# Retention of a two-layer network: results kept heads by tokens, score groups over four banks, value products of eight heads in one visit

## Chip, cores, metric
One core of a Trainium2 chip runs the kernel. The time is the device time in microseconds (us) of one execution. All data are fp32.

## What is computed
`reference` applies two layers to x (32 x 256 x 128): first a mean-field attention with a gated feed-forward, then the layer that the change touches, a retention with 16 heads and a mixture of 8 experts with soft routing. The retention, cut to what matters:

```python
qk = x @ W_qk + b_qk;  v = x @ W_v + b_v              # 16 heads, 8 wide (q, k), 16 wide (v)
scores = einsum('bhtd,bhsd->bhts', q, k) * mask       # causal decay, divided by a row scale
denom = clip(abs(scores).sum(-1), 1.0, 50000.0)
ret = einsum('bhts,bhsv->bthv', scores / denom, v)
ret = ret * rsqrt(mean(ret * ret, -1) + EPS)          # over the 16 values of a head
gated = (x @ W_g + b_g) * ret.reshape(Bx, Tx, H * VD)
return gated @ W_o + b_o
```

Both the old and the new kernel use that dividing by `denom` and then normalizing is u / sqrt(mean(u*u) + EPS*denom*denom) for the undivided u.

## The kernel before
The sequences are worked on in 16 pairs, 512 tokens (4 tiles of 128) each. The steps of all stages are short functions, one per engine and step; the table `ORDER` lists for each engine the order of its steps as (name, index, age). `steps_of` runs through that list once per cycle, 18 times in all (`pairs + ages`), and a step of age 1 or 2 works on the pair of one or two cycles ago. So each engine interleaves the first layer of pair p with the second layer of pair p-1 and the end of pair p-2, in an order written out by hand. Every engine works its list strictly in order; semaphores (`filled`, `ready`) tie the lists together.

PSUM has four single banks, `banks`, which the steps share by the table `BANK`, and `bank_s` of four banks for the scores. `claim` (line 812) makes TensorE wait until the last step that used a bank has been read, by the table `READ_BY`.

The retention of a pair, before (32 units: 2 sequences with 16 heads; a group `q` of 4 heads, 8 groups):
- `qk`, `vg` (L908, L913): projections; `qkc` (L644, VectorE) adds the bias and the decay, `vgc` (L652, L654) puts values and gates into `vrow` and `grow`, tokens by heads. `km` (L323, GpSimd) masks k to one head of each 32-row group.
- `quad` (L990, L993, TensorE): scores of 4 heads at once, one per 32-row group, each into a bank of `bank_s`: 256 query columns for the first 128 keys, 128 columns for the second. `ret` (L661, VectorE) multiplies by the causal block into one of two buffers, `ab` (L485, ScalarE) takes the absolute value, `add` (L329, GpSimd) adds the parts of it.
- `g` (L1008, TensorE): per head and 32-column group, values times `ret` (256 and 128 columns) and a column of ones times `ret_abs` (256), 4 heads in a bank. `RTc` (L490) copies it out; `row` (L1018) turns four of these back to tokens by heads.
- `usq` (L495), `rowd` (L670 to L677) and `urs` (L334, a power -0.5 on GpSimd) make the factor per head and token; `gated` (L683), `gatedT` (L1027) turned again, `gTc` (L500), `o` (L1035) and `attn` (L691).
The expert part is `xn3T`, `LT` (L920), `DT` (L942), `slots` (L950), `h` (L959), `eo` (L969), `out` (L979) on TensorE with `LTc`, `DTe`, `Dc`, `slc`, `ce` and `hg` (L480, Gelu) on ScalarE, `LTm`, `mx`, `cs`, `hb` (L726), `eoc`, `z` on VectorE and `dn` (L340) on GpSimd. The first layer has `xnT`, `s`, `e`, `k`, `r`, `v`, `score`, `PT`, `srow`, `local`, `xn2T` on TensorE, and `mix` (L556) among VectorE's steps.

Of the kernel before, what the change touches and what calls it, by code (L numbers as in the profile page):

```python
# [32 lines left out]
def columns(*widths):  # L33
    out, at = {}, 0
    for name, n in widths:
# [25 lines left out]
           ("row", 2, 1), ("gatedT", 0, 1), ("row", 3, 1), ("out", 0, 1), ("xn2T", 0, 0), ("out", 1, 1)],  # L61
    "DVE": [("z", 1, 2), ("stat", 0, 0), ("qkc", 0, 1), ("qkc", 1, 1), ("gated", 2, 2), ("vgc", 0, 1),
            ("LTm", 0, 1), ("LTm", 1, 1), ("ret", 0, 1), ("drec", 0, 1), ("attn", 0, 2), ("gated", 3, 2),
            ("vgc", 1, 1), ("xn", 0, 0), ("drec", 1, 1), ("LTm", 2, 1), ("zg", 0, 2), ("ret", 1, 1),
            ("attn", 1, 2), ("mx", 0, 1), ("LTm", 3, 1), ("drec", 2, 1), ("vgc", 2, 1), ("mx", 1, 1), ("mx", 2, 1),
            ("drec", 3, 1), ("vgc", 3, 1), ("ret", 2, 1), ("rmax", 0, 1), ("ret", 3, 1), ("cs", 0, 1),
            ("cs", 1, 1), ("mix", 0, 0), ("cs", 2, 1), ("ret", 4, 1), ("gbias", 0, 0), ("hb", 0, 1),
            ("rowd", 0, 1), ("hb", 1, 1), ("ret", 5, 1), ("hb", 2, 1), ("rowd", 1, 1), ("hb", 3, 1), ("eoc", 0, 1),
            ("sg", 0, 2), ("hb", 4, 1), ("ka", 0, 0), ("smax", 0, 0), ("eoc", 1, 1), ("smax", 1, 0),
            ("gated", 0, 1), ("ret", 6, 1), ("srowc", 0, 0), ("hb", 5, 1), ("ret", 7, 1), ("rv", 0, 0),  # L70
# [55 lines left out]
def build(nc, x, weights, vectors, consts, w1, w2, slot_rows, out):  # L126
    pairs = x.shape[0] // TOK
    ages = max(age for order in ORDER.values() for _, _, age in order)
    with ExitStack() as ctx:
# [45 lines left out]
        RT = sb("RT", 4, SEQ)
        usq = sb("usq", 2, HEADS, VD)
        ug, gated = sb("ug", TILES, HEADS, VD), sb("gated", 2, HEADS * VD)
        ums, den, den2, uvar, urs = (sb(n, TILES, HEADS) for n in ("ums", "den", "den2", "uvar", "urs"))
        gatedT = sb("gatedT", 2, 2, 2, P)
# [943 lines left out]
```

## Time and profile before

| | |
|---|---|
| time, median of 3 runs | 1098.42 us (1098.21 to 1098.63) |
| profiled execution, its time / span | 1098.24 us / 1096.4 us |
| busy: TensorE, VectorE, ScalarE, GpSimd | 1062.8, 960.2, 773.0, 606.9 us |
| mean granted TensorE clock | 0.992 of full speed |

The engine names in rows: PE is the matmul side of TensorE, PEld its weight loads, DVE VectorE, ACT ScalarE, POOL GpSimd. A matrix product in fp32 leaves two records each for product and load; ends of products are modelled, so that the distance from one start to the next is what a step takes. L-numbers are lines of the kernel. In a row, `128*32 128x256` is stationary rows*columns, then what streams.

### The profile page before, as it was taken

How to read it: one execution, taken by the hardware profiler on the slowest of the kernel's cores; microseconds unless marked ns; L12 is line 12 of the kernel's file. 1: busy time of each engine (PE TensorE's matmuls, PEld its weight loads, DVE VectorE, ACT ScalarE, POOL GpSimd, SP SyncE). 2: the span in 40 equal slices, each digit the busy share in tenths (PEclk: the TensorE clock that was granted, in tenths of full speed). 3: DMA queues.
4: the chain of work that ended last, by engine and by line, in shares of the span. 5: the costliest groups of instructions: out<-in, count | busy, mean ns of one | idle time of the engine just before them, and what ended most of it. 6: DMA issues, size and time to landing. Idle time of an engine off the chain costs nothing.

```text
span 1096.4 us, 27975 instructions
## 1 busy us (share of the span) xinstructions
PE 1062.8 (97%) x10436; PEld 832.9 (76%) x10436; DVE 960.2 (88%) x2074; ACT 773.0 (71%) x1450; POOL 606.9 (55%) x619
## 2 busy tenths in 40 slices
PE   5799999999999999999999999999999999999997
PEld 3478687787868778687787868778687787868776
DVE  3788989899898988989899898988989899898985
ACT  3476786767777676786767777676786767777674
POOL 2465547556474665547556474655647556474553
PEclk9899999999999999999999999999999999999998
DMA  6000000000000000000000000000000000000000
GB/s 257 11 2 11 1 20 3 1 21 1 21 1 11 11 1 22 1 12 10 2 21 1 21 1 2 20 2 21 2 11 11 2 20 2 21 1 2 11 1 20
DMA packets 18468, 16.97 MB, mean 15 GB/s; under 512 B 800, under 2 KB 17440, under 8 KB 18080
## 3 DMA queue, kind: packets, MB, share of 16 engines
q1 hardware_dynamic: 18336, 15.18, 4.2%
q8 instruction: 86, 1.41, 0.6%
q14 instruction: 46, 0.38, 0.1%
HBM read 10.98 MB, written 4.19 MB: 14 GB/s over the span
## 4 chain that ended last, share of the span: by engine, by line
PE 90%; DVE 6%; issue 1%; ACT 1%; POOL 0%; POOLq 0%; DVEq 0%; ACTq 0%
PE bank L1008 12%; PE bank L959 11%; PE bank L969 10%; PE bank_s L990 7%; PE bank L950 5%; PE bank L979 5%; PE bank L920 5%; PE bank L913 5%; PE bank L1035 3%; DVE ret L661 3%; PE bank L908 3%; PE bank L823 3%; PE bank L874 3%; PE bank L1018 3%; PE bank_s L993 2%; PE bank L854 2%
## 5 line engine op out<-in xcount | busy, mean ns | idle before, releaser
L329 POOL TENSOR_TENSOR ret_abs<-ret_abs 128x512 f32<-128x512 f32 x128 | 168.7, 1318 | 238.2 <-ACT ret_abs L485 238.2
L661 DVE TENSOR_TENSOR ret<-bank_s,k_sb 128x1536 f32<-128x1536 f32 x128 | 223.9, 1749 | 23.7 <-PE bank L1008 14.8
L334 POOL TENSOR_TENSOR urs<-uvar,mhalf 128x16 f32<-128x16 f32 x64 | 185.3, 2903 | 91.8 <-DVE uvar L677 91.8
L485 ACT ACTIVATE ret_abs<-ret 128x1536 f32<-128x1536 f32 x128 | 189.6, 1481 | 8.8 <-DVE ret L661 8.8
L959 PE MATMUL bank<-slotsT,w_sb 128*128 128x128 f32 x1024 | 140.9, 281 | 0.3 <-DVE hact L726 0.3
L969 PEld LDWEIGHTS bank<-w_sb,hact 128*128 128x128 f32 x1024 | 125.5, 192 | 14.7 <-issue 13.9
L969 PE MATMUL bank<-w_sb,hact 128*128 128x128 f32 x1024 | 134.1, 277 | 0.0
L959 PEld LDWEIGHTS bank<-slotsT,w_sb 128*128 128x128 f32 x1024 | 124.3, 192 | 10.3 <-issue 7.4
L340 POOL TENSOR_SCALAR dT<-dT,drec 128x256 f32<-128x256 f32 x128 | 83.4, 665 | 48.6 <-DVE drec L721 48.4
L1008 PE MATMUL bank<-ret,vrow 128*32 128x256 f32 (+1 forms) x2048 | 108.6, 329 | 0.3 <-DVE hact L726 0.2
L990 PE MATMUL bank_s<-qT,km 32*128 32x256 f32 x1024 | 91.4, 426 | 5.0 <-DVE ret L661 5.0
L726 DVE TENSOR_TENSOR hact<-bank,v_sb 128x512 f32<-128x512 f32 x128 | 87.4, 684 | 6.7 <-PE bank L959 5.3
L1008 PEld LDWEIGHTS bank<-ret,vrow 128*32 128x32 f32 x2048 | 59.7, 109 | 42.7 <-issue 5.0
L480 ACT ACTIVATE hact<-hact 128x512 f32<-128x512 f32 x128 | 79.8, 624 | 8.1 <-DVE hact L726 7.8
L446 ACT ACTIVATE cT<-bank 128x512 f32<-128x512 f32 x64 | 38.2, 597 | 58.1 <-PE bank L920 55.8
L1008 PE MATMUL bank<-ret_abs,k_sb 128*32 128x256 f32 x1024 | 79.2, 379 | 0.0
L990 PEld LDWEIGHTS bank_s<-qT,km 32*128 32x128 f32 x1024 | 40.4, 183 | 50.4 <-issue 48.2
L490 ACT ACTIVATE RT<-bank 128x256 f32<-128x256 f32 x128 | 48.0, 375 | 40.6 <-PE bank L1008 40.6
L323 POOL TENSOR_SCALAR km<-kT,k_sb 128x256 f32<-128x256 f32 x128 | 69.5, 543 | 6.9 <-DVE kT L644 6.8
L913 PE MATMUL bank<-w_sb,xn2T 128*128 128x512 f32 x128 | 66.1, 598 | 0.0
L461 ACT ACTIVATE dT<-cT,ltmax 128x256 f32<-128x256 f32 x128 | 64.0, 509 | 0.0
L979 PE MATMUL bank<-eorow,cT 128*128 128x129 f32 x512 | 62.3, 275 | 0.0
(143 smaller groups left out, 2397.9 us busy)
## 6 DMA issues: line engine op xcount, KB each, us to landing
x_sb<-x SPq DMA_DIRECT2D x16, 256.0 KB, 2.8
w_sb<-w SPq DMA_DIRECT2D x2, 2048.0 KB, 14.8
out<-attn SPq DMA_DIRECT2D x16, 256.0 KB, 2.3
v_sb<-vectors SPq DMA_DIRECT2D x1, 832.0 KB, 8.1
w_sb<-weights SPq DMA_DIRECT2D x1, 512.0 KB, 5.3
k_sb<-consts SPq DMA_DIRECT2D x1, 466.0 KB, 6.6
w_sb<-weights SPq DMA_DIRECT2D x1, 320.0 KB, 3.2
slot_sb<-slot_rows SPq DMA_DIRECT2D x1, 256.0 KB, 3.5
```

Source lines behind the costliest of these rows:

```text
L329: pool.tensor_tensor(both[:, :, P:SEQ], both[:, :, P:SEQ], both[:, :, SEQ:3 * P], ALU.add)\
L334: pool.tensor_tensor(urs[:, j], uvar[:, j], mhalf[:], ALU.pow).then_inc(ready["urs"].sem, 1)
L340: ins = pool.tensor_scalar(dT[:, m % 2, b], dT[:, m % 2, b], drec[:, m, b:b + 1], 1.0, ALU.mult, ALU.mult)
L485: act.activation(ret_abs[:, q % MR], ret[:, q % MR], ACT.Abs).then_inc(ready["ab"].sem, 1)
L661: dve.tensor_tensor(ret[:, q % MR], bank_s[:, :, 0:3 * P], causal.unsqueeze(1).broadcast_to([P, Q, 3 * P]), ALU.mult)\
L726: dve.tensor_tensor(hact[:, e % 2], bank[:].rearrange("p (c n) -> p c n", c=HC), V["b1"][:, e * HC:(e + 1) * HC].unsqueeze(2).broadcast_to ...
L913: pe.matmul(bank[:], xn2T[:, j // 2, (j % 2) * P:(j % 2 + 1) * P], W["vg"], start=True, stop=True)\
L959: ins = pe.matmul(bank[:, c * P:(c + 1) * P], w1_sb[:, e, c * P:(c + 1) * P], slotsT[:, e // 2, 2 * (e % 2):2 * (e % 2) + 2].rearrange("p ...
L969: ins = pe.matmul(bank[:, i * C:(i + 1) * C], hact[:, i, c], w2_sb[:, e, c], start=(c == 0), stop=(c == HC - 1))
L979: ins = pe.matmul(bank[:, i * (C + 1):(i + 1) * (C + 1)], cT[:, m, j * P:(j + 1) * P], eorow[:, m, b], start=(m == 0), stop=(m == E // 2 - 1))
L990: pe.matmul(bank_s[:, n, 0:SEQ], km[rows, q % KM, 0:P], qT[par][rows, b], start=True, stop=True)
L1008: ins = pe.matmul(bank[n * HT:(n + 1) * HT, sblock * P:SEQ], left, src[:, q % MR, n, cols[0]:cols[1]], start=(phase == 0), stop=(phase == 2))
```

## The change
The retention is laid out anew, and the order of all engines with it.
- Scores: `scores` (named "A") comes in six visits per pair, three per sequence. The first fills `bank_s` with the 128-column parts of all 16 heads (`low`); the second and third with the 256-column parts of 8 heads each (`high`). `ret` and `ab` now handle 2048 elements per partition, in one buffer each; `add` handles 1024.
- Values: `values` ("gg") takes eight heads in one visit of a bank. A head has 16 rows: the left half of the bank holds u for 8 heads by 256 tokens, the right half the sum of |scores|, spread over the head's 16 rows. `row`, `RTc`, `gatedT`, `gTc` are gone; `gT` and `gTb` make the gates heads by tokens as well.
- Norm: `ms` multiplies the squares by a block matrix (1/16 within a head) into the right half; `den`, `dsq`, `rx` add EPS*denom^2; `ln` and `rs` form exp(-0.5 ln) on ScalarE for a whole pair at once, in place of the powers `urs` on GpSimd.
- The orders of PE, DVE, ACT and POOL and the table `BANK` are new. `xn2T`, `eo 6`, `eo 7` and `out` move to the start of the next cycle.

```diff
-    "PE": [("qk", 0, 1), ("xn3T", 0, 1), ("qk", 1, 1), ("vg", 0, 1), ("LT", 0, 1), ("LT", 1, 1), ("quad", 0, 1),
...
+    "PE": [("xn2T", 0, 1), ("eo", 6, 2), ("eo", 7, 2), ("qk", 0, 1), ("qk", 1, 1), ("out", 0, 2), ("xn3T", 0, 1),
+           ("out", 1, 2), ("LT", 0, 1), ("xnT", 0, 0), ("A", 0, 1), ("s", 0, 0), ("o", 0, 2), ("LT", 1, 1),
+           ("A", 1, 1), ("LT", 2, 1), ("vg", 0, 1), ("o", 1, 2), ("LT", 3, 1), ("k", 0, 0), ("gT", 0, 1),
+           ("gT", 1, 1), ("DT", 0, 1), ("DT", 1, 1), ("A", 2, 1), ("gg", 0, 1), ("DT", 2, 1), ("DT", 3, 1),
+           ("vg", 1, 1), ("slots", 0, 1), ("slots", 1, 1), ("global", 0, 0), ("ms", 0, 1), ("mxT", 0, 1),
+           ("h", 0, 1), ("gg", 1, 1), ("A", 3, 1), ("rB", 0, 1), ("e", 0, 0), ("h", 1, 1), ("r", 0, 0),
+           ("A", 4, 1), ("h", 2, 1), ("eo", 0, 1), ("h", 3, 1), ("eo", 1, 1), ("ms", 1, 1), ("score", 0, 0),
+           ("score", 1, 0), ("srow", 0, 0), ("A", 5, 1), ("gg", 2, 1), ("PT", 0, 0), ("PT", 1, 0), ("v", 0, 0),
+           ("eo", 2, 1), ("local", 0, 0), ("eo", 3, 1), ("ms", 2, 1), ("h", 4, 1), ("h", 5, 1), ("h", 6, 1),
+           ("gg", 3, 1), ("eo", 4, 1), ("h", 7, 1), ("eo", 5, 1), ("ms", 3, 1)],
...
+    "DVE": [("eoc", 2, 2), ("xn3", 0, 1), ("eoc", 3, 2), ("stat", 0, 0), ("qkc", 0, 1), ("qkc", 1, 1), ("z", 0, 2),
+            ("xn", 0, 0), ("gated", 0, 2), ("gated", 1, 2), ("z", 1, 2), ("LTm", 0, 1), ("ret", 0, 1),
+            ("mix", 0, 0), ("attn", 0, 2), ("drec", 0, 1), ("LTm", 1, 1), ("ret", 1, 1), ("drec", 1, 1),
+            ("vgc", 0, 1), ("zg", 0, 2), ("attn", 1, 2), ("LTm", 2, 1), ("sg", 0, 2), ("mx", 0, 1), ("LTm", 3, 1),
...
+    "ACT": [("hg", 7, 2), ("xn2Tc", 0, 1), ("ln", 0, 2), ("rs", 0, 2), ("xn3Tc", 0, 1), ("LTc", 0, 1),
+            ("xnTc", 0, 0), ("DTe", 0, 1), ("sT", 0, 0), ("zt", 0, 2), ("LTc", 1, 1), ("ab", 0, 1), ("DTe", 1, 1),
+            ("LTc", 2, 1), ("ab", 1, 1), ("kr", 0, 0), ("gTb", 0, 1), ("LTc", 3, 1), ("DTe", 2, 1), ("Dc", 0, 1),
...
-        ret, ret_abs = sb("ret", MR, Q, 3 * P), sb("ret_abs", MR, Q, 3 * P)
...
+        low, low_abs = sb("low", Q, Q, P), sb("low_abs", Q, Q, P)
+        high, high_abs = sb("high", Q, 2, SEQ), sb("high_abs", Q, 2, SEQ)
...
+            def ln(p, par, k):
+                act.wait_ge(*ready["rx"](p, DUOS - 1))
+                act.activation(rx[:], rx[:], ACT.Ln).then_inc(ready["ln"].sem, 1)
+
+            def rs(p, par, k):
+
+                act.wait_ge(*ready["ln"](p))
+                act.activation(rx[:], rx[:], ACT.Exp, scale=-0.5).then_inc(ready["rs"].sem, 1)
...
+            def ret_(p, par, a):
+                b, i = divmod(a, 3)
+                dve.wait_ge(*filled["A"](p, a))
...
+                    since(dve, filled["gg"], *((p, h - 1) if h else (p - 1, HALVES - 1)))
+                    ins = dve.tensor_tensor(high[:].rearrange("p n i m -> p (n i) m"), flat.rearrange("p (u m) -> p u m", m=SEQ),
+                                            causal[:, 0:SEQ].unsqueeze(1).broadcast_to([P, 2 * Q, SEQ]), ALU.mult)
...
+            def rx_(p, par, h):
+                dve.wait_ge(*filled["ms"](p, h))
+                dve.wait_ge(*ready["dsq"](p, h))
+                dve.wait_ge(*ready["ug"](p, h))
+                since(dve, ready["gated"], p - 1, h // 2)
+                dve.tensor_tensor(rx[:, h], banks[BANK["gg", h]][:, SEQ:], den[:, h % 2], ALU.add).then_inc(ready["rx"].sem, 1)
...
+                for u, q in enumerate(quads):
                     for n in range(Q):
-                        src = (ret, ret_abs)[phase // 2]
...
+                        rows = slice(n * HT, (n + 1) * HT)
+                        if i == 0:
+                            ins = pe.matmul(bank_s[:, n, u * P:(u + 1) * P], km[rows, q % KM, P:SEQ], qT[par][rows, b, P:SEQ],
+                                            start=True, stop=True)
+                        else:
+                            ins = pe.matmul(bank_s[:, n, u * SEQ:(u + 1) * SEQ], km[rows, q % KM, 0:P], qT[par][rows, b],
+                                            start=True, stop=True)
+                ins.then_inc(filled["A"].sem, 1)
...
+                for i in range(2):
+                    for phase in range(3):
+                        for n in range(Q):
...
+                            right = (high[:, n, i], low[:, n, 2 * half + i], high_abs[:, n, i])[phase]
+                            into = ((0, SEQ), (P, SEQ), (SEQ, 2 * SEQ))[phase]
+                            ins = pe.matmul(bank[n * HT:(n + 1) * HT, into[0]:into[1]], left, right,
+                                            start=(i == 0 and phase == 0), stop=(i == 1 and phase == 2))
...
+            def ms(p, par, h):
+                pe.wait_ge(*ready["den"](p, h))
+                pe.wait_ge(*ready["ug"](p, h))
+                pe.matmul(banks[BANK["gg", h]][:, SEQ:], K["heads"], usq[:, h % 2], start=True, stop=True)\
+                  .then_inc(filled["ms"].sem, 1)
```

## Rows read from the trace of the kernel before

**Rows 1.** The page: part 1 busy us of engines; part 2 granted clock.
```profile
PE 1062.8 (97%) x10436; PEld 832.9 (76%) x10436; DVE 960.2 (88%) x2074; ACT 773.0 (71%) x1450; POOL 606.9 (55%) x619
...
PEclk9899999999999999999999999999999999999998
```

**Rows 2.** Timeline of PE: start us, us, instructions; first `qk` of two cycles.
```profile
103.74 1.02 PE L908 MATMUL bank<-xn2T,w_sb 128*128 128x512 f32 x2
...
499.46 1.02 PE L908 MATMUL bank<-xn2T,w_sb 128*128 128x512 f32 x2
```

**Rows 3.** Two cycles: us, busy of PE, PEld, DVE, ACT, POOL; clock, DMA.
```profile
499.46:565.40 65.94, 65.67 (x655) 51.75 (x653) 59.75 (x129) 48.06 (x90) 37.75 (x39) 1.00 0.03 10
565.40:631.34 65.94, 65.65 (x652) 51.51 (x651) 59.65 (x127) 48.05 (x90) 37.51 (x39) 1.00 0.04 10
```

**Rows 4.** Waits of PE from 499 to 631 us: total us, times, longest.
```profile
PE bank_s L990 <- DVE ret L661: 0.5, 2, 0.3
```

**Rows 5.** Timeline of PE within the cycle from 499.46 us.
```profile
503.77 0.59 PE L920 MATMUL bank<-xn3T,slot_sb 128*128 128x256 f32 x2
504.30 0.71 PE L990 MATMUL bank_s<-qT,km 32*128 32x256 f32 x8
...
505.16 1.16 PE L1035 MATMUL bank<-w_sb,gatedT 128*128 128x128 f32 x8
...
520.05 0.71 PE L990 MATMUL bank_s<-qT,km 32*128 32x256 f32 x8 [0.28 <-DVE ret L661]
...
530.17 0.60 PE L1018 MATMUL bank<-k_sb,RT 128*128 128x128 f32 x4
530.62 1.13 PE L959 MATMUL bank<-slotsT,w_sb 128*128 128x128 f32 x8
...
543.78 0.86 PE L1008 MATMUL bank<-ret,vrow 128*32 128x256 f32 x16
...
546.08 1.16 PE L959 MATMUL bank<-slotsT,w_sb 128*128 128x128 f32 x8
```

**Rows 6.** Timeline of the weight loads in the same visit.
```profile
504.62 0.42 PEld L993 LDWEIGHTS bank_s<-qT,km 32*128 32x128 f32 x8
```

**Rows 7.** Groups by line, PE: records, busy us, mean ns | idle before.
```profile
L1018 PE MATMUL bank<-k_sb,RT 128*128 128x128 f32 x256 | 38.8, 274 | 0.0
...
L1027 PE MATMUL bank<-k_sb,gated 128*128 128x128 f32 x128 | 19.3, 273 | 1.7 <-DVE gated L683 1.7
```

**Rows 8.** Groups by line, the other engines.
```profile
L661 DVE TENSOR_TENSOR ret<-bank_s,k_sb 128x1536 f32<-128x1536 f32 x128 | 223.9, 1749 | 23.7 <-PE bank L1008 14.8 <-PE bank_s L993 8.9
L485 ACT ACTIVATE ret_abs<-ret 128x1536 f32<-128x1536 f32 x128 | 189.6, 1481 | 8.8 <-DVE ret L661 8.8
L334 POOL TENSOR_TENSOR urs<-uvar,mhalf 128x16 f32<-128x16 f32 x64 | 185.3, 2903 | 91.8 <-DVE uvar L677 91.8
L329 POOL TENSOR_TENSOR ret_abs<-ret_abs 128x512 f32<-128x512 f32 x128 | 168.7, 1318 | 238.2 <-ACT ret_abs L485 238.2
...
L726 DVE TENSOR_TENSOR hact<-bank,v_sb 128x512 f32<-128x512 f32 x128 | 87.4, 684 | 6.7 <-PE bank L959 5.3
...
L480 ACT ACTIVATE hact<-hact 128x512 f32<-128x512 f32 x128 | 79.8, 624 | 8.1 <-DVE hact L726 7.8
...
L480 ACT ACT_TABLE_LOAD x32 | 41.1, 1283 | 0.6
L455 ACT ACT_TABLE_LOAD x32 | 41.1, 1283 | 0.6
...
L671 DVE TENSOR_TENSOR ug<-bank,grow 128x256 f32<-128x256 f32 x64 | 26.5, 415 | 0.0
```

**Rows 9.** Instructions of line 556: ns shortest/median/longest, first and last start.
```profile
L556 DVE SCALAR_TENSOR_TENSOR mix<-xnT,v_sb,mix x32: 744/961/1752, 11.2 to 989.0; 128x512 f32<-128x512 f32 x32
```

**Rows 10.** The chain that ended last, near its end: start us, us.
```profile
1082.08 2.91 POOL urs L334
1084.99 2.88 POOLq L129
```

More of the change, by code:

```diff
@@ L50 @@
 ORDER = {
[10 rows of a table removed]
[L61 to L70, printed above, removed]
[3 rows of a table removed]
@@ L102 @@
+BANK = {("DT", 0): 3, ("DT", 1): 2, ("DT", 2): 3, ("DT", 3): 1, ("LT", 0): 1, ("LT", 1): 0, ("LT", 2): 3,
[5 rows of a table added]
+        ("score", 0): 2, ("score", 1): 3, ("slots", 0): 1, ("slots", 1): 3, ("srow", 0): 1, ("v", 0): 3,
+        ("vg", 0): 2, ("vg", 1): 2, ("xn2T", 0): 2, ("xn3T", 0): 1, ("xnT", 0): 3}
 READ_BY = {"xnT": ("xnTc", 0), "s": ("sT", 0), "global": ("gbias", 0), "e": ("eTc", 0), "srow": ("srowc", 0),
            "score": "P", "PT": "PTc", "local": ("field", 0), "r": ("tr", 0), "k": ("kr", 0), "v": ("rv", 0),
-           "xn2T": ("xn2Tc", 0), "xn3T": ("xn3Tc", 0), "qk": "qkc", "vg": "vgc", "LT": "LTc", "mxT": ("rmax", 0), "rB": ("rBc", 0), "DT": "Dc", "slots": "slc", "h": "hb", "eo": "eoc", "row": "ug", "g": "RTc", "gatedT": "gTc", "o": "attn",
+           "xn2T": ("xn2Tc", 0), "xn3T": ("xn3Tc", 0), "qk": "qkc", "vg": "vgc", "LT": "LTc", "mxT": ("rmax", 0), "rB": ("rBc", 0), "DT": "Dc", "slots": "slc", "h": "hb", "eo": "eoc", "gg": "rx", "gT": "gTb", "o": "attn",
@@ L170, in build @@
         qT, kT = ([sb(f"{n}_{i}", 2, SEQ) for i in range(2)] for n in ("qT", "kT"))
-        KM, MR = 4, 2
+        KM = 4
         km = sb("km", KM, SEQ)
-        vrow, grow = sb("vrow", TILES, HEADS, HT), sb("grow", TILES, HEADS, VD)
-        ret, ret_abs = sb("ret", MR, Q, 3 * P), sb("ret_abs", MR, Q, 3 * P)
[L175 to L179, printed above, removed]
+        vrow, grow = sb("vrow", TILES, HEADS, HT), sb("grow", 2, TOK)
+        low, low_abs = sb("low", Q, Q, P), sb("low_abs", Q, Q, P)
+        high, high_abs = sb("high", Q, 2, SEQ), sb("high_abs", Q, 2, SEQ)
+        usq, den = sb("usq", 2, SEQ), sb("den", 2, SEQ)
+        ug, rx = sb("ug", DUOS, SEQ), sb("rx", DUOS, SEQ)
         attn = sb("attn", TILES, C)
@@ L214, in build @@
             ("prod", 1), ("x1", 1), ("stat2", 1), ("mv2", 1), ("var_eps2", 1), ("rstd2", 1), ("rn", 3), ("rnorm", 1),
-            ("xn2", 1), ("xn3", 1), ("xn2Tc", 1), ("xn3Tc", 1), ("qkc", 2), ("km", QUADS), ("vgc", 4), ("ret", QUADS),
-            ("ab", QUADS), ("add", QUADS), ("RTc", QUADS), ("usq", 4), ("ug", 4), ("den", 4), ("den2", 4), ("ums", 4),
-            ("uvar", 4), ("urs", 4), ("gated", 4), ("gTc", 2), ("attn", 2), ("LTc", 4), ("mx", 3), ("rmax", 1), ("rBc", 1), ("cs", 4), ("ce", 4),
+            ("xn2", 1), ("xn3", 1), ("xn2Tc", 1), ("xn3Tc", 1), ("qkc", 2), ("km", QUADS), ("vgc", 2), ("gTb", 2), ("ret", GROUPS),
+            ("ab", GROUPS), ("add", HALVES), ("usq", DUOS), ("den", DUOS), ("dsq", DUOS), ("ug", DUOS),
+            ("rx", DUOS), ("ln", 1), ("rs", 1), ("gated", 2), ("attn", 2), ("LTc", 4), ("mx", 3), ("rmax", 1), ("rBc", 1), ("cs", 4), ("ce", 4),
             ("ltmax", 4), ("DTe", 4), ("drec", 4), ("dn", 4), ("Dc", 4), ("slc", 2), ("hb", E), ("hg", E),
@@ L492, in usq_, with ab @@
[L492 to L501 removed]
+            def ab(p, par, a):
+                b, i = divmod(a, 3)
+                act.wait_ge(*ready["ret"](p, a))
+                if i == 0:
+                    since(act, ready["add"], *((p, 1) if b else (p - 1, 3)))
+                    ins = act.activation(low_abs[:], low[:], ACT.Abs)
+                else:
+                    h = 2 * b + i - 1
+                    since(act, filled["gg"], *((p, h - 1) if h else (p - 1, HALVES - 1)))
+                    ins = act.activation(high_abs[:], high[:], ACT.Abs)
+                ins.then_inc(ready["ab"].sem, 1)
@@ new lines, in gTb, with usq_ @@
+            def gTb(p, par, u):
+                bank = bank_of("gT", p, u)
+                since(act, ready["ug"], p - 1, 2 + u)
+                act.activation(grow[:, u], bank[:], ACT.Identity, bias=V["b_g"][:, u:u + 1]).then_inc(ready["gTb"].sem, 1)
+            def usq_(p, par, h):
+                act.wait_ge(*filled["gg"](p, h))
+                since(act, filled["ms"], *((p, h - 2) if h >= 2 else (p - 1, h + 2)))
+                act.activation(usq[:, h % 2], banks[BANK["gg", h]][:, 0:SEQ], ACT.Square).then_inc(ready["usq"].sem, 1)
@@ new lines, in den_, with ug_ @@
+            def den_(p, par, h):
+                dve.wait_ge(*ready["usq"](p, h))
+                since(dve, ready["rx"], *((p, h - 2) if h >= 2 else (p - 1, h + 2)))
+                dve.tensor_scalar(den[:, h % 2], banks[BANK["gg", h]][:, SEQ:], 1.0, 50000.0, ALU.max, ALU.min)\
+                   .then_inc(ready["den"].sem, 1)
+            def ug_(p, par, h):
+                b, u = divmod(h, 2)
+                dve.wait_ge(*ready["usq"](p, h))
+                dve.wait_ge(*ready["gTb"](p, u))
+                since(dve, filled["o"], p - 1, b)
+                dve.tensor_tensor(ug[:, h], banks[BANK["gg", h]][:, 0:SEQ], grow[:, u, b * SEQ:(b + 1) * SEQ], ALU.mult)\
+                   .then_inc(ready["ug"].sem, 1)
@@ L1012, in row @@
[L1012 to L1028 removed]
+                pe.wait_ge(*ready["km"](p, quads[-1]))
```

224 lines of the change are left out of this document (85 added, 139 removed), and 36 rows, old and new, of tables (BANK, ORDER).

## The prediction
> **What bounds the kernel now.** I read the busy shares and the clock first, then one pair of sequences in the middle, then what TensorE waits for. TensorE is busy 97% of the span and the granted clock is full (2.4 GHz) in nearly every slice [rows 1]. The kernel repeats one cycle for each of 16 pairs; from 103.74 to 499.46 us are six cycles, so 65.95 us each [rows 2]. In two neighbouring cycles TensorE is busy 65.7 of 65.94 us, VectorE 59.7, ScalarE 48.1, GpSimd 37.6 [rows 3], and the only wait of TensorE on another engine is for `ret`, 0.5 us in two cycles [rows 4]; with the 0.16 us in which the engine picks up afterwards that is about 0.4 us a cycle [rows 5], a visit at 520.05 after 0.28 us idle. So TensorE's instruction stream is the bound: a microsecond less of it per pair is worth 16 us, as long as VectorE, which has 6 us to spare, and the order allow it.
>
> **TensorE, part by part (per pair).** Step times are taken from start to start, since the ends are modelled [rows 5].
> - Score visits. A `quad` streams 256 and 128 columns in four row groups at once; from 504.30 to 505.16 it takes 0.86 us, and about 0.1 us is lost before it, because the half `LT` at 503.77 takes 0.53 where 0.43 is usual [rows 5]. Two full-width products of 128 rows by 256 columns take 0.86 (LT), so 256 columns cost 0.43 and 384 would cost 0.64; the remaining 0.22 inside is the entry and the exit. Old: 8 x 0.64 = 5.12 of streaming. New: each of six visits fills four banks with 512 columns per row group, 0.86: 5.16. The streaming is the same; what goes is two visits with 0.22 inside and some 0.2 around each: 0.8 less.
> - Value visits. A pair of `g` takes 2.30 (543.78 to 546.08) for 2 x (256+128+256) columns. One new visit of `values` streams the same 1280 columns in four column groups: 2.30, four of them as before. No change.
> - `row` is four transposes, 0.45 (530.17 to 530.62); `gatedT` is the same form with the same mean of about 273 ns a record [rows 7]. Four and two of them go: 2.7 less.
> - `ms` is added, one product of 128x128 with 256 columns, 0.43: four, 1.7 more.
> - `vg` was four visits of 512 columns; now `vg` is two with 2 x 256 and `gT` two with 512: 3.4 before and after. `o` has the same four products, from `ug` instead of `gatedT`: nothing.
> Sum: -0.8 -2.7 +1.7 = -1.8, and -2.2 if the 0.4 of waiting goes too. A packed TensorE would have a cycle of 63.7.
>
> **The other engines (per pair).** VectorE: 8 `ret` at 1.75, 20 half-bank steps (vrow, grow, ug, ums, gated) at 0.415 and 12 of 16 elements, taken as 0.2, are 24.7; new are 6 `ret` of 2048 elements. The 1536-element row (1749 ns) and the 512-element row `hb` (684 ns) give 1.04 ns an element, so 2.28 each; 12 half-bank steps (den, ug, rx) at 0.415; two `vgc` and two `gated` of 512 elements at 0.70: 21.5. That is 3.2 less [rows 8]. A step with two operands in SBUF is longer while GpSimd works beside it: one step of `mix` takes 0.74 us at its shortest, and 0.96 in the median [rows 9]. ScalarE: 1481 ns at 1536 and 624 ns at 512 elements give 1.91 us at 2048, 1.05 at 1024 and 0.41 at 256 [rows 8]. Out go 8 Abs, 8 RTc and 4 usq of 256, 2 gTc of 512: 18.0. In come 6 Abs, 2 gTb of 512, 4 usq and 4 dsq of 256, `ln` and `rs` of 1024: 18.1, and table loads. No row shows Ln. Every pair now loads a table four times, 1.283 us each [rows 8], in two lines of 32 loads; the bound below is none more, the one above is three more (for ln, for rs, for the next Tanh), and I take one more, because rs and the following DTe are Exp alike and Ln is one stray function. That makes ScalarE 1.4 longer, about 50 of 65. The Trainium skill (ScalarE: Activation LUTs, Table sets) lists one set that holds both exp and ln, and does not name tanh in it; by it there is one load more as well, and no run here shows it yet. GpSimd: 4 `urs` at 2.9 and 8 adds at 1.32 go; 4 adds of 1024 elements come, between 1.32 (no growth) and 2 x 1.32 = 2.6, taken as 2.5, since the old one is almost all streaming: 38 becomes 26 [rows 8].
>
> **Where new waits come.** `low` and `high` have one buffer each where `ret` had two, so a visit of `values` now waits for one unbroken chain: score visit, ret 2.28, Abs 1.91, add 2.5, hand-overs of 0.15; and the next `ret` of `high` waits for that value visit. The chain with its visit is 9.3 us; four of them are 37 of 64, so it is no bound as such, only where the order sets it too close. I therefore laid the new order out by hand from the row times, TensorE's steps end to end from `xn2T` = 0, and the steps of VectorE, ScalarE and GpSimd between them where their inputs are ready.
> - First, batch 0: `A1` ends at 14.3; VectorE then still has mix, attn and LTm, so ret1 runs 15.5 to 17.8, Abs to 19.9, add to 22.4; TensorE reaches the visit at 22.95. 0.4 to spare. Here `mix` counts 1.4 for its two steps, since GpSimd has nothing that is ready then; at up to 1.75 each, ret1 is 2.1 later and this visit 1.7 late.
> - Second: ret2 must wait for that visit (25.4) and ends at 27.7, Abs 29.6, add 32.1; the visit comes at 32.9. 0.7 to spare.
> - Third: ret4 40.8 to 43.1, Abs 45.0, add 47.5; the visit at 48.2. 0.6 to spare. Fourth: ret5 ends 53.3, add 57.7; the visit at 59.2.
> - Waits found elsewhere: `k` wants bank 3, which LTc2 reads only after Abs 0 and DTe1 on ScalarE: 0.5. `mxT` wants bank 2 from vgc1, which stands behind `ret2`: 0.1. The third value visit wants bank 0, which `rx1` frees behind smax0 and cs0: 0.2. The end (usq3, den3, ug3, hb6, xn2, hb7, rx3 behind the fourth visit, then `xn2T`, `eo7`) fits within 0.2.
> Together 1.0 us of the packed cycle's saving is given back: 64.8. `ln` and `rs` lie between xn2Tc and xn3Tc with TensorE in `out` until 6 us: even three loads more end before xn3T is done, so they are priced at nothing; if that cover fails, a load costs at most 1.3 a cycle.
>
> **From the profiled run to the time.** The run took 1098.24 for a span of 1096.4, and the median is 1098.42. The cycle is 1.15 shorter sixteen times: -18.4. The tail after the last output product had two powers on GpSimd in a row, 2.91 and 2.88 [rows 10]; instead come ln, rs, one or two loads, and four expert products and `out` that now lie behind the last value visit: -2 to +2, taken as -1. 1098.4 - 18.4 - 1 = 1079.
>
> **Rivals.**
> - Packed TensorE: the waits I found are errors of half a microsecond in a layout, and nothing delays it. For it: before, nearly nothing delayed it at 91% of VectorE busy, and now VectorE is at 87%. Against: the single buffers. 2.2 x 16 = 35, and the tail: 1062.
> - Slower, by the chain score, ret, Abs, add, values. If the four value visits each come 0.5 us later than laid out (`mix` or another step of VectorE at its long form ahead of `ret`, an add above 2.6), a cycle is 66.8, and 0.86 x 16 = +14, tail -1: 1111. It decides at 0.29 us per visit beyond the spare time of 0.4 to 0.7, so hand-overs or add must be 0.7 to 1.0 us worse than priced. For it: the spare is thin in three of four places. Against: in the trace Abs and add are steady, and GpSimd is left with much less to do.
> - Slower through weight loads. The low visit has sixteen products of 128 columns, thus twice the loads for each column of the high one. If a load could not run under a product of its own row group, each of 8 rounds would take 0.107 + 0.107: 0.86 more for each of two low visits, a cycle of 66.5: 1106. Against it: in the old visit the loads of L993 begin at 504.62, under the products of L990 [rows 5, 6]. The Trainium skill (TensorE: Matmul & The Clock Gate, Part 3) says that loads overlap running products only when the row group differs, and in Part 2 allows a background buffer; the row speaks for the latter.
> - The change does not pay: the given-back time is all of it, 1096 to 1100; or most of it, 1088 to 1096.
>
> **Chances.** Forecast (1071 to 1088) 0.43, packed (1060 to 1071) 0.23, most given back (1088 to 1096) 0.12, nothing left (1096 to 1100.6) 0.06, slower by the chain 0.12, slower by loads 0.04. A difference of 0.2%, 2 us, is about what a measurement of this kernel can tell. Faster 0.78, same 0.06, slower 0.16. The range goes from packed, with some room for the tail, to past no change: 1060 to 1102. It leaves out some 0.03 below and 0.13 above.
>
> **What would show it.** Cycle of 64 to 65.5 us between first products of `qk`; TensorE busy near 64; score visits of 1.05 to 1.1 us, both kinds alike (a low visit of 1.9 is the load rival); value visits of 2.3; adds near 2.5; ret 2.28, Abs 1.91; five table loads a pair. TensorE's waits should name LTc or a bank's reader, some tenths each, not POOL's add; if value visits wait for the add, the chain rival holds. Wrong altogether it would be if VectorE were busy over 95% in a cycle, or if the granted clock fell below full speed in these gaps.

## The result: 1107.48 us, slower where faster was forecast

| | before | after |
|---|---|---|
| median | 1098.32 us (1097.97 to 1098.63) | 1107.48 us (1105.87 to 1108.13) |
| ratio to before | 1 | 1.0081 (1.0064 to 1.0099) |
| profiled execution, its time / span | 1098.24 / 1096.4 us | 1107.50 / 1105.6 us |
| cycle of one pair | 65.95 us | 66.45 us |

The time lies above the range of 1060 to 1102. The page of the kernel after, against [rows 1]: busy us of the engines, and the engines' shares of the chain of work that ended last.

```profile
PE 1046.7 (95%) x10244; PEld 817.5 (74%) x10244; DVE 931.0 (84%) x1786; ACT 806.6 (73%) x1402; POOL 372.1 (34%) x491
...
PEclk9899999999999999999999999999999999999999
...
PE 49%; DVE 37%; issue 10%; ACT 3%; POOL 1%; POOLq 0%; DVEq 0%; DMA 0%; ACTq 0%
```

TensorE has less to do, as forecast, and the granted clock is 0.994 of full speed (0.992 before); but 37% of the chain runs through VectorE, which is busy for only 84% of the span. Two cycles of after, columns as in [rows 3] (us, busy of PE, PEld, DVE, ACT, POOL):

```profile
432.55:499.00 66.45, 64.75 (x643) 50.89 (x642) 58.06 (x111) 50.18 (x88) 23.00 (x30) 1.00 0.03 10
499.00:565.45 66.45, 64.76 (x643) 50.90 (x642) 58.08 (x111) 50.20 (x88) 23.00 (x30) 1.00 0.03 9
```

Before, TensorE was idle for 0.27 us of a cycle [rows 3]; now for 1.70. VectorE is at 58.1, where 59.75 - 3.2 = 56.6 was expected. What TensorE waits for over the whole execution (total us, times, longest), against the single kind of wait in [rows 4]:

```profile
PE bank L971 <- POOL dT L337: 13.1, 16, 0.9
PE bank L844 <- DVE xn L639: 11.9, 16, 7.0
PE bank L1044 <- DVE rx L701: 9.8, 16, 2.7
```

Three waits come in each of the 16 pairs: the last `DT`, `xn2T` at the start of the cycle (one of its 16 is 7.0, at the start of the program), and the third visit of `values`. The wait of a value visit for the add, which the forecast feared, is 0.3 us in the whole execution. The chain that ended last (start us, us, what) names in every cycle a step that the prediction didn't mention:

```profile
449.86 2.86 DVE attn L779
...
516.30 2.88 DVE attn L779
```

L779 is the VectorE step `sg` (gate times the first layer's result; both operands in SBUF). Groups by line of after (busy us, mean ns), and below them the same step in the kernel before:

```profile
L330 POOL TENSOR_TENSOR high_abs<-high_abs,low_abs 128x1024 f32<-128x1024 f32 x64 | 151.3, 2364 | 390.3 <-ACT high_abs L489 390.1
...
L779 DVE SCALAR_TENSOR_TENSOR attn<-attn,zt 128x512 f32<-128x512 f32 x16 | 43.7, 2730 | 0.0
...
L618 DVE SCALAR_TENSOR_TENSOR prob<-prob 128x512 f32<-128x512 f32 x16 | 18.2, 1140 | 0.5
...
L587 DVE TENSOR_SCALAR snmax<-smax 128x2 f32<-128x2 f32 x32 | 14.1, 442 | 1.1
```

```profile
L758 DVE SCALAR_TENSOR_TENSOR attn<-attn,zt 128x512 f32<-128x512 f32 x16 | 11.1, 693 | 0.5
```

`sg` takes 2730 ns where it took 693, with the same operands. The timeline says why. VectorE, then GpSimd, then TensorE of after in the cycle that starts at 499.00 (start us, us, instructions, in brackets the idle time before):

```profile
515.70 0.67 DVE L717 TENSOR_REDUCE ltmax<-cT 128x2 f32<-128x512 f32 x1
516.30 2.88 DVE L779 SCALAR_TENSOR_TENSOR attn<-attn,zt 128x512 f32<-128x512 f32 x1
519.09 0.68 DVE L726 TENSOR_TENSOR mx<-cT 128x512 f32<-128x512 f32 x1
519.70 0.67 DVE L717 TENSOR_REDUCE ltmax<-cT 128x2 f32<-128x512 f32 x1
```

```profile
516.25 2.37 POOL L330 TENSOR_TENSOR high_abs<-high_abs,low_abs 128x1024 f32<-128x1024 f32 x1
520.64 0.93 POOL L337 TENSOR_SCALAR dT<-dT,drec 128x256 f32<-128x256 f32 x2 [2.02 <-DVE drec L742]
```

```profile
523.15 0.66 PE L971 MATMUL bank<-k_sb,dT 128*128 128x128 f32 x4 [0.86 <-POOL dT L337]
...
545.86 0.64 PE L1044 MATMUL bank<-high,vrow 128*32 128x256 f32 x8 [0.47 <-DVE rx L701]
...
562.88 0.66 PE L844 MATMUL bank<-k_sb,xn 128*128 128x128 f32 x4 [0.33 <-DVE xn L639]
```

The add of GpSimd starts at 516.25, `sg` 0.05 us later. The add ends at 518.62; `sg` ends at 519.18, which is 0.56 later, about its own working time. So it stood for the whole add. Behind it wait `mx` 0, `LTm` 3 (519.70), the exponential on ScalarE, the reciprocal, `dn` 3 on GpSimd and the last `DT` of TensorE (523.15). My theory was from here on: **a VectorE step with two operands in SBUF does nothing while GpSimd's add, which reads SBUF, is running; the add is now one instruction of 2.36 us, and the order puts such steps under it.** The rivals: the tighter order would make TensorE wait anyway; the table loads; the TensorE stream itself is longer than priced.

### The profile page after: what moved, and what is told of

The parts are those of the page before. It is cut to its first block, busy times and chain, and to the rows that moved or that the text cites. A ratio compares the mean times of both kernels' runs of the same rounds, so it can differ in the third digit from the quotient of the medians.

```text
span 1105.6 us, 27048 instructions
## 1 busy us (share of the span) xinstructions
PE 1046.7 (95%) x10244; PEld 817.5 (74%) x10244; DVE 931.0 (84%) x1786; ACT 806.6 (73%) x1402; POOL 372.1 (34%) x491
## 4 chain that ended last, share of the span: by engine, by line
PE 49%; DVE 37%; issue 10%; ACT 3%; POOL 1%; POOLq 0%; DVEq 0%; DMA 0%; ACTq 0%
PE bank L998 8%; PE bank L988 8%; PE bank L1044 7%; PE bank L979 5%; DVE attn L779 4%; DVE hact L747 3%; DVE ltmax L717 3%; DVE high L678 3%; PE bank L895 3%; DVE stat L545 2%; DVE xn L561 2%; DVE eorow L758 2%; DVE low L673 2%; PE bank_s L1025 2%; PE bank_s L1022 2%
## 5 line engine op out<-in xcount | busy, mean ns | idle before, releaser
L330 POOL TENSOR_TENSOR high_abs<-high_abs,low_abs 128x1024 f32<-128x1024 f32 x64 | 151.3, 2364 | 390.3 <-ACT high_abs L489 390.1
L678 DVE TENSOR_TENSOR high<-bank_s,k_sb 128x2048 f32<-128x2048 f32 x64 | 146.1, 2283 | 24.0 <-PE bank_s L1025 20.7
L489 ACT ACTIVATE high_abs<-high 128x2048 f32<-128x2048 f32 x64 | 122.3, 1911 | 33.6 <-DVE high L678 32.2
L673 DVE TENSOR_TENSOR low<-bank_s,k_sb 128x2048 f32<-128x2048 f32 x32 | 73.3, 2291 | 34.6 <-PE bank_s L1022 34.6
L1044 PE MATMUL bank<-high,vrow 128*32 128x256 f32 x1024 | 81.7, 387 | 10.1 <-DVE rx L701 9.8
L1044 PE MATMUL bank<-high_abs,k_sb 128*32 128x256 f32 x1024 | 80.8, 381 | 0.0
L1008 PEld LDWEIGHTS bank<-eorow,cT 128*128 128x128 f32 x512 | 60.8, 192 | 8.3 <-issue 8.3
L485 ACT ACTIVATE low_abs<-low 128x2048 f32<-128x2048 f32 x32 | 61.0, 1908 | 5.9 <-DVE low L673 5.9
L844 PE MATMUL bank<-k_sb,xn 128*128 128x128 f32 x256 | 40.7, 283 | 19.7 <-DVE xn L639 11.9
L979 PE MATMUL bank<-d,xn 128*128 128x512 f32 x128 | 58.7, 601 | 0.0
```

Of the source, the lines that this page charges most:

```text
L330: pool.tensor_tensor(high_abs[:, :, :, P:SEQ], high_abs[:, :, :, P:SEQ], low_abs[:, :, 2 * half:2 * half + 2], ALU.add)\
L489: ins = act.activation(high_abs[:], high[:], ACT.Abs)
L673: ins = dve.tensor_tensor(low[:].rearrange("p n i m -> p (n i) m"), flat.rearrange("p (u m) -> p u m", m=P), causal[:, 2 * P:3 * P].unsque ...
L678: ins = dve.tensor_tensor(high[:].rearrange("p n i m -> p (n i) m"), flat.rearrange("p (u m) -> p u m", m=SEQ), causal[:, 0:SEQ].unsqueeze ...
L979: ins = pe.matmul(bank[:], xn3[:, j], d[:, j], start=(i == 0), stop=(i == 1))
L1008: ins = pe.matmul(bank[:, i * (C + 1):(i + 1) * (C + 1)], cT[:, m, j * P:(j + 1) * P], eorow[:, m, b], start=(m == 0), stop=(m == E // 2 - 1))
```

## The experiments

Ratios are to the kernel before on the same chip, with a 95% interval; all edits but the last are to the kernel after.

**e1: `LTm` 3 goes ahead of `sg`.**

```diff
-("LTm", 2, 1), ("sg", 0, 2), ("mx", 0, 1), ("LTm", 3, 1),
+("LTm", 2, 1), ("LTm", 3, 1), ("sg", 0, 2), ("mx", 0, 1),
```

> One swap in VectorE's order: LTm 3 (one operand) goes ahead of sg and mx 0 (two operands in SBUF). Theory A, collision: sg was issued at 516.30 into GpSimd's add (516.25 to 518.62) and stood until the add was over (2.88 us for a step of 0.69), and TensorE's wait of 0.86 for the last dn came from it; with the swap sg starts as the add ends and takes 0.7 to 0.9, the wait before the last DT goes, a cycle is 65.5 instead of 66.45, about 1092. Theory B, chain of score, ret, Abs, add, values: nothing of it is touched, 1107. Theory C, VectorE has just too much work in this stretch: the work is the same in another order, 1104 to 1107.

Measured: 1096.46 us, 0.9986 (0.9976 to 0.9995). `sg`, and the wait of `DT` over the whole execution:

```profile
L779 DVE SCALAR_TENSOR_TENSOR attn<-attn,zt 128x512 f32<-128x512 f32 x16 | 11.9, 747 | 0.0
```

```profile
PE bank L971 <- POOL dT L337: 0.3, 1, 0.3
```

One exchange of steps, with no work changed, gives some 11 us back: the cycle goes from 66.45 to 65.65, where 65.5 and 1092 us were expected. The first of the three waits is gone; the two others remain (11.8 and 9.7 us).

**e2: the add as two instructions of 512 elements.**

```diff
-pool.tensor_tensor(high_abs[:, :, :, P:SEQ], high_abs[:, :, :, P:SEQ], low_abs[:, :, 2 * half:2 * half + 2], ALU.add)
+for n in (slice(0, 2), slice(2, 4)):
+    ins = pool.tensor_tensor(high_abs[:, n, :, P:SEQ], high_abs[:, n, :, P:SEQ], low_abs[:, n, 2 * half:2 * half + 2], ALU.add)
```

> GpSimd's add of 1024 elements is made in two instructions of 512, with the same work and one signal at the end. Theory A with the refinement that a blocked step gets in when the running instruction ends: sg takes 1.6 to 1.9 instead of 2.73 in the mean, and the wait for the last dn is gone or below 0.2: 1093 to 1100. If the block lasts as long as GpSimd has adds queued, sg stays at 2.8 to 3.0 and the time at 1107 to 1109. Theory B: the add is 0.1 longer in the chain, 1107 or a little more.

Measured: 1111.34 us, 1.0116 (1.0099 to 1.0132); the mean of `sg` is 1708. VectorE and GpSimd in one cycle (line numbers are one higher here):

```profile
520.44 1.78 DVE L780 SCALAR_TENSOR_TENSOR attn<-attn,zt 128x512 f32<-128x512 f32 x1
522.15 1.75 DVE L727 TENSOR_TENSOR mx<-cT 128x512 f32<-128x512 f32 x1
```

```profile
520.40 2.95 POOL L331 TENSOR_TENSOR high_abs<-high_abs,low_abs 128x512 f32<-128x512 f32 x2
```

`sg` is let in between the halves, so the step stands for one instruction of GpSimd and not for all that it has queued. But the second half then holds the next two-operand step, `mx` 0, for another 1.1 us, and `LTm` 3 starts 3.43 us after the add's start (523.83), where it was 3.45 with the whole add. The blocking did what the theory says; that halving would save time (1093 to 1100 expected) was wrong. Against the kernel after, the cycle is 0.27 longer: TensorE comes 0.13 later to the third value visit, and another 0.14 to the fourth.

**e3: the add over one column only.** It leaves out the second block's part of the sum of |scores|.

```diff
-pool.tensor_tensor(high_abs[:, :, :, P:SEQ], high_abs[:, :, :, P:SEQ], low_abs[:, :, 2 * half:2 * half + 2], ALU.add)
+pool.tensor_tensor(high_abs[:, :, :, P:P + 1], high_abs[:, :, :, P:P + 1], low_abs[:, :, 2 * half:2 * half + 2, 0:1], ALU.add)
```

> The add on GpSimd covers one column in place of 128 in each block, so the sum of absolute scores leaves out the second block's part: work is left out, and the wait order stays. Theory A: sg 0.69, snmax 0.17, prob 0.7 to 1.0, TensorE waits below 1 us a cycle, cycle 64.6 to 65.0, 1078 to 1084. Theory B would give the same direction, but then the waits that vanish are those of the value visits. Theory C: VectorE busy would stay at 58 in a cycle, and the time above 1100.

Measured: 1077.58 us, 0.9811 (0.9792 to 0.9831), so 29.9 less than the kernel after. Under theory A 1078 to 1084 was expected. All three waits have gone together, and the blocked steps are short (`rvg`, L618, whose rows say prob, has 692 ns too):

```profile
L779 DVE SCALAR_TENSOR_TENSOR attn<-attn,zt 128x512 f32<-128x512 f32 x16 | 11.4, 713 | 0.0
...
L587 DVE TENSOR_SCALAR snmax<-smax 128x2 f32<-128x2 f32 x32 | 5.4, 169 | 1.1
```

This removes the duration of the add, too, and so doesn't yet tell blocking from a chain that is shorter by 2.1 us. e6 does.

**e4 and e5: the orders around the other two waits.** e4 is e1 with `rx` 1 ahead of `cs` 0 and `hb` 4 ahead of `rvg`; e5 is e4 with `P` 1 ahead of `ce` 0 on ScalarE, for a wait of 5.8 us for the output of ScalarE's step `P` (prob in the rows) that e4 showed.

```diff
-("smax", 0, 0), ("cs", 0, 1), ("rx", 1, 1), ("smax", 1, 0),
+("smax", 0, 0), ("rx", 1, 1), ("cs", 0, 1), ("smax", 1, 0),
...
-("rvg", 0, 0), ("hb", 4, 1), ("rx", 2, 1),
+("hb", 4, 1), ("rvg", 0, 0), ("rx", 2, 1),
...
-("P", 0, 0), ("ce", 0, 1), ("P", 1, 0), ("usq", 2, 1),
+("P", 0, 0), ("P", 1, 0), ("ce", 0, 1), ("usq", 2, 1),
```

> Three swaps in VectorE's order: LTm 3 ahead of sg; rx 1 ahead of cs 0, so that bank 0 is free for the third value visit (TensorE waited 0.47 for it); hb 4 ahead of rvg, which stood in the fourth add for 1.17 us. Theory A plus the late bank: waits of 0.9, 0.5 and up to 0.5 of the end of the cycle go, cycle 64.6 to 65.0, 1078 to 1085. Theory B: 1105 to 1107. Theory C: 1100 to 1107.

> The three swaps of e4_three_swaps, and in ScalarE's order both P steps ahead of ce 0: in that run TensorE waited 0.37 for the second P, and the second PT began 1.03 us after the first. Theory A (collisions and late hand-overs near them make up what the change gave back): the wait goes, 0.4 to 0.5 a cycle, 1082 to 1085 against 1089.4. If VectorE is the bound of that stretch, as its idle time below 0.3 us there suggests, the wait only moves to xn2T at the end of the cycle: 1088 to 1090.

Measured: e4 1089.36 us, 0.9919 (0.9904 to 0.9934), a cycle of 65.37, and so outside the 1078 to 1085 that were expected; e5 1083.80 us, 0.9867 (0.9853 to 0.9882), as expected. TensorE's waits in e4, and then in e5, where that for `xn` is down to what comes once per execution, that for `rx` is not listed any more, and that for prob is 0.4, once:

```profile
PE bank L885 <- ACT prob L399: 5.8, 16, 0.4
```

```profile
PE bank L844 <- DVE xn L639: 7.0, 1, 7.0
...
PE bank L885 <- ACT prob L399: 0.4, 1, 0.4
```

`snmax` is still held in e5 (442 ns in the mean), and ScalarE waits for it: the table load of `P` begins 0.07 us after the end of `snmax` (534.53 in one cycle). The group of these loads in e5, with ScalarE's idle time ahead of them as the last number:

```profile
L399 ACT ACT_TABLE_LOAD x15 | 19.2, 1283 | 6.9 <-issue 6.9
```

That is 0.46 us a cycle in after, e4 and e5, and 0.3 us in the whole execution of e3 and of e6, in which TensorE waits only once for prob (0.3 and 0.2 us) though `ce` 0 stands between the two `P`. So the fourth exchange makes up for a delay that, by these two runs, comes from the held `snmax`. With the full work done, e5 is 1.3% faster than the kernel before and 23.7 us faster than the change as it was made: four exchanges gave back most of what the adds cost.

**e6: in place of the add, a memset of the same buffer.** It leaves out the whole sum of |scores|, since it overwrites what was there. A memset writes SBUF and reads nothing; it takes 1.81 us.

```diff
-pool.tensor_tensor(high_abs[:, :, :, P:SEQ], high_abs[:, :, :, P:SEQ], low_abs[:, :, 2 * half:2 * half + 2], ALU.add)
+pool.memset(high_abs[:], 1.0)
```

> The changed kernel with its own order; each add on GpSimd is replaced by a memset of 2048 elements of its result tile, some 1.8 us long by the memset of that size in the trace: the sum of the absolute scores is left out. GpSimd is as busy nearly as long at the same places, but reads nothing. If a two-operand step of VectorE stands because GpSimd is reading from SBUF, sg takes 0.69 to 0.75 and the time is that of e3_no_add, 1077 to 1080. If any use of SBUF by GpSimd blocks it, sg takes 1.9 to 2.5 and the time is 1095 to 1103.

Measured: 1077.38 us, 0.9810 (0.9790 to 0.9829). VectorE and GpSimd at the place where `sg` stood before:

```profile
504.36 0.68 DVE L779 SCALAR_TENSOR_TENSOR attn<-attn,zt 128x512 f32<-128x512 f32 x1
504.96 0.68 DVE L726 TENSOR_TENSOR mx<-cT 128x512 f32<-128x512 f32 x1
```

```profile
504.28 1.80 POOL L330 MEMSET high_abs<- 128x2048 f32 x1
```

`sg` starts 0.08 us behind GpSimd's instruction (0.05 in the kernel after), both steps lie wholly under it, and neither is longer. So it isn't that GpSimd is at work, nor that it writes: what is left is that the add reads. (A memset is also another kind of instruction; but the last section shows `dn`, which is no add either and reads SBUF, and it does hold such a step.) And with 1.8 us of GpSimd work in the chain of each value visit the time is that of e3; the chain isn't what costs. For `snmax` and `rvg` this run says less: the memset is over when they begin, but for 0.14 and 0.03 us. Whether a memset of the add's full 2.36 us would have held them isn't shown.

**e7: no table loads for the norm.** Abs in place of Ln and Exp, the power -0.5 is left out.

```diff
-act.activation(rx[:], rx[:], ACT.Ln)
+act.activation(rx[:], rx[:], ACT.Abs)
...
-act.activation(rx[:], rx[:], ACT.Exp, scale=-0.5)
+act.activation(rx[:], rx[:], ACT.Abs, scale=-0.5)
```

> The changed kernel with Abs in place of Ln and of Exp in ln and rs, which need no table of their own: the power -0.5 is left out. Two loads of 1.283 us a pair go from ScalarE (and none is needed for the next Exp beyond those of the old order: 3 to 4 a pair instead of 5). Prediction and theory A: they are hidden behind out on TensorE, 1105.5 to 1108. A rival is that they delay xn3Tc and LTc 0 and so all that follows: 1.3 to 2.6 a cycle, 1066 to 1087.

Measured: 1106.94 us, 1.0081 (1.0064 to 1.0098), a cycle of 66.43: the same as after. ScalarE is 28.4 us less busy, and it buys nothing. The run shows something else. VectorE, then GpSimd:

```profile
516.22 0.68 DVE L779 SCALAR_TENSOR_TENSOR attn<-attn,zt 128x512 f32<-128x512 f32 x1
516.82 2.85 DVE L726 TENSOR_TENSOR mx<-cT 128x512 f32<-128x512 f32 x1
```

```profile
516.32 2.79 POOL L330 TENSOR_TENSOR high_abs<-high_abs,low_abs 128x1024 f32<-128x1024 f32 x1 [0.15 <-ACT high_abs L489]
```

Here `sg` comes 0.10 ahead of the add and is short, and `mx` 0 behind it is held to the add's end plus 0.56. The add in turn is 0.43 longer than its 2.36. So whichever starts first goes on and the other stands, in both directions, and `LTm` 3 is as late as before. The loss doesn't hang on 0.05 us of luck; it hangs on which kinds of steps stand there.

**e8: the kernel before, with its add over one column only** (the same part of the sum left out).

```diff
-pool.tensor_tensor(both[:, :, P:SEQ], both[:, :, P:SEQ], both[:, :, SEQ:3 * P], ALU.add)
+pool.tensor_tensor(both[:, :, P:P + 1], both[:, :, P:P + 1], both[:, :, SEQ:SEQ + 1], ALU.add)
```

> The kernel before with its add on GpSimd cut to one column (the second block's absolute scores are left out of the sum). Theory A says that the old kernel had as many collisions, but covered: mix and mx fall to 0.75 and 0.70 from 1.32 and 1.17 in the mean, VectorE is busy some 2 us less a cycle, and the time hardly moves, since TensorE waited only 0.4 a cycle: 1091 to 1098. If collisions cost the old kernel as much as the new one (29 us), the time would be near 1070.

Measured: 1086.57 us, 0.9893 (0.9878 to 0.9908); more than was expected. The group of `mix` in the kernel before, and in e8:

```profile
L556 DVE SCALAR_TENSOR_TENSOR mix<-xnT,v_sb,mix 128x512 f32<-128x512 f32 x32 | 40.9, 1316 | 21.2 <-POOL mix L297 21.2
```

```profile
L556 DVE SCALAR_TENSOR_TENSOR mix<-xnT,v_sb,mix 128x512 f32<-128x512 f32 x32 | 25.9, 852 | 11.9 <-POOL mix L297 11.9
```

The old kernel had the same trouble, 11.7 us of it, with adds of 1.32 each. The wait for `ret` of [rows 4] (5.0 us in the whole execution) is gone in e8, and its cycle is 65.4. This edit shortens the add as well, and no run with a memset parts the two for the old kernel; that the steps were held there is seen in their lengths (`mx` 1 and 2 from 1167 to 692 ns, `rvg` from 1022 to 682, `snmax` from 284 to 170). So the adds cost the old layout 0.6 us a cycle and the new one 1.9 (66.45 to e6's 64.56). Without the adds the new layout is 9.0 us faster than the old one (1077.58 to 1086.57).

## Why the prediction was wrong, point by point

In short: 1079 us was forecast and 1107.5 measured. The step that failed is the one that priced the new waits at 1.0 us a cycle with every step of VectorE at its unhindered length; the adds on GpSimd hold such steps, and that costs 1.89 us a cycle, 30 us. TensorE's sum was off by another 1.0 a cycle, which was made up for by waits that are nearly none once the adds are out.

**TensorE's sum: right in sign, 1.0 us a cycle too favourable.** e8 and e6 are both nearly packed (65.36 and 64.53 busy in cycles of 65.36 and 64.56), so that their steps, summed from start to start, show each term. `row` and `gatedT`: 2.72 away (-2.7 forecast). Value visits: 9.21 and 9.21 (no change forecast). Scores: 6.93 to 6.52, -0.4 where -0.8 was taken: the old visit was priced with 0.2 around it that its neighbours don't get back. `ms`: 1.91 where 1.7 was taken, since of its four products some meet a neighbour at 0.5. `xn2T` is 0.68 in e6 where four transposes take 0.43 elsewhere; the rest is tenths at new boundaries. The sum is -0.8 where -1.8 was forecast. Single durations were right: this is after, low score visit and high one (start to start 1.10 and 1.07, forecast 1.05 to 1.1), and the first value visit (2.31, forecast 2.30):

```profile
506.12 1.17 PE L1022 MATMUL bank_s<-qT,km 32*128 32x128 f32 x32
507.22 1.12 PE L854 MATMUL bank<-xnT,w_sb 128*128 128x512 f32 x2
...
510.04 1.15 PE L1025 MATMUL bank_s<-qT,km 32*128 32x256 f32 x16
511.11 0.70 PE L949 MATMUL bank<-xn3T,snT 128*128 128x256 f32 x2
...
519.32 0.64 PE L1044 MATMUL bank<-high,vrow 128*32 128x256 f32 x8
...
521.63 0.66 PE L971 MATMUL bank<-k_sb,dT 128*128 128x128 f32 x4
```

So the rival of the weight loads is false: a low visit is not 0.86 longer than a high one.

**"Where new waits come": the step that failed.** The layout by hand put every VectorE step in at the length of its unhindered row, with one exception. The rows for the other one had been read ("a step with two operands in SBUF is longer while GpSimd works beside it" [rows 9]) and were applied to `mix` alone, and there only because GpSimd would be idle. `sg`, `mx` and `rvg` are such steps too (and `snmax` behaves like one), and it was not asked what GpSimd runs beside them. The add had been priced rightly at 2.5 (2.36), as a delay of the value visits; that it stops VectorE for as long was not priced at all. In the layout `LTm` 3 was 2.2 us too early by that (2.88 less 0.69), and the chain `LTm`, `DTe`, `drec`, `dn`, `DT` has no such spare. Of the four waits that were listed, the one of `k` didn't come (it starts 0.87 after the `LT` step ahead of it, as packed), for `mxT` the trace names none, the third value visit's came at 0.5 instead of 0.2, and the end's at 0.33 with what follows it instead of 0.2. Against e6 the cycle of after is 0.95 longer at the last `DT`, 0.54 ahead of the third value visit and 0.39 ahead of `xn2T`: 1.88 of the 1.89.

**The forecast number.** Packed 63.7 and 1.0 of waits gave 64.8 and 1079. Without the adds the cycle is 64.56 and the time 1077.4. That is near, but by luck, since two errors cancel: the packed cycle is 64.5, not 63.7, and the waits are nearly none, not 1.0. To it come 1.89 x 16 = 30 us that no term of the sum contained. What lies outside the 16 cycles is 1107.5 - 1063.2 = 44.3, against 43.2 before: +1 where -1 was taken, inside its bounds.

**The other engines.** `high` and `low` took 2283 and 2291 ns (2.28 forecast), Abs 1911 and 1908 (1.91). The lines that the prediction priced for VectorE come to 24.3 a pair in e8 and 21.3 in e3 (24.7 and 21.5 forecast), so that sum held. VectorE's busy time as a whole fell by only 2.0 a cycle (57.2 in e8, 55.2 in e3): `xn`, which no term had, went from 361 to 476 ns, since it now stands beside `km` of GpSimd (last section), and that is 0.45; what makes up the rest stays open. The adds put 2.5 on the old one and 2.9 on the new. ScalarE is at 50.2 ("about 50"), GpSimd at 23.0 (26 forecast). The table loads are five a pair, as forecast and for its reason:

```profile
L508 ACT ACT_TABLE_LOAD x16 | 20.5, 1283 | 0.3
...
L513 ACT ACT_TABLE_LOAD x16 | 20.5, 1283 | 0.3
```

`ln` and `rs` load each, and the Exp of `DTe` behind them finds its table there. The Trainium skill (ScalarE: Activation LUTs, Table sets) lists a set with exp and ln together, by which `rs` would have needed none; the trace shows one, and the measurement decides. That the loads are hidden was right: e7.

**The rivals.** "Slower, by the chain score, ret, Abs, add, values" named the right sign and even nearly the right time (1111), by a mechanism that didn't occur: TensorE waits 0.3 us for the add in the whole execution, and in e6 1.8 us of GpSimd in the same chain cost nothing. Its aside on a step of VectorE "at its long form" was nearest to the truth, but it looked for it ahead of `ret`. The last sentence ("if VectorE were busy over 95% in a cycle, or if the granted clock fell below full speed") was no test: neither happened, VectorE is at 87% of a cycle, and yet it was its order that ended last.

## What to carry to other kernels

Where an order is laid out by hand, mark the VectorE steps with two operands in SBUF, and those like `snmax` and `xn` that read one tensor in SBUF and write SBUF, and the GpSimd instructions that read SBUF. Let no step that others wait for lie among or behind the first while the second runs; here steps that read PSUM, and reductions, kept their length in such places. Fusing two of GpSimd's adds into one lengthened the time for which one holds VectorE from 1.32 to 2.36 us, and halving it back doesn't help where two such steps stand in a row. A low busy share of both engines says nothing on this: look in the groups for a step whose mean is far above its shortest or above that of its equals.

## What the runs showed of the hardware

- A two-operand VectorE step that starts 0.05 us after GpSimd's add stands until the add ends: 2.88 us instead of 0.69 (after). If it starts first, the add stands: 2.79 instead of 2.36 (e7). Beside a memset of 1.80 us it takes 0.68 (e6). The Trainium skill (SBUF — State Buffer, SBUF: two separate sides) says that VectorE and GpSimd share a pair of ports by an exclusive lock which the first holds for its whole instruction; that on VectorE's side it concerns operations in a 2-port performance mode and those with two SBUF inputs; and that the latter are concerned only by a GpSimd one that reads SBUF. For the steps with two inputs the trace agrees: one waits for the whole add, the other order makes the add longer, and the memset holds nothing.
- It isn't only the add. `mx` 1 starts in e5 while one half of `dn`, a GpSimd step of 0.48 us that reads SBUF, is running (511.02 to 511.50), and takes 0.86 instead of 0.69. The other half, which comes 0.31 behind `mx` 1, in turn takes 0.91. VectorE, then GpSimd:

```profile
511.17 0.86 DVE L726 TENSOR_TENSOR mx<-mx,cT 128x512 f32<-128x512 f32 x1
```

```profile
511.48 0.91 POOL L337 TENSOR_SCALAR dT<-dT,drec 128x256 f32<-128x256 f32 x1
```

- It isn't only steps with two tensors. The last three of the four parts of `xn` take 0.54 us each in e6, where the first takes 0.34, and start 0.45 us apart, beside four `km` of GpSimd that start at the same distance:

```profile
491.43 1.70 DVE L561 TENSOR_SCALAR xn<-x_sb,mv,rstd 128x128 f32<-128x128 f32 x4
```

```profile
491.21 1.84 POOL L323 TENSOR_SCALAR km<-kT,k_sb 128x256 f32<-128x256 f32 x4 [0.31 <-DVE kT L656]
```

  And `snmax`, which changes 128x2 elements in SBUF, is held too. VectorE, then GpSimd, in after:

```profile
543.31 0.69 DVE L584 TENSOR_REDUCE smax<-bank 128x2 f32<-128x512 f32 x1
544.04 0.74 DVE L587 TENSOR_SCALAR snmax<-smax 128x2 f32<-128x2 f32 x1
...
546.34 0.17 DVE L587 TENSOR_SCALAR snmax<-smax 128x2 f32<-128x2 f32 x1
```

```profile
542.39 2.36 POOL L330 TENSOR_TENSOR high_abs<-high_abs,low_abs 128x1024 f32<-128x1024 f32 x1 [13.44 <-ACT high_abs L489]
```

  Under the add it takes 0.74 and ends when the add does (544.75); free of it, 0.17. The reduction just ahead reads PSUM and has its usual length under the same add. In which mode `snmax` and `xn` run, no trace shows.
- Of the 0.44 us a cycle between e5 (65.00) and e6 (64.56), TensorE loses 0.17 at the last `DT` and 0.16 ahead of `xn2T`, in both places behind steps of VectorE that the exchanges had moved, and 0.1 between them. What stays open is how much an order would give that keeps all such steps away from the adds; none was tried.
